# A fifth unit's input product on GpSimd, softplus summed by TensorE, and a re-timed step schedule in a bidirectional selective-scan kernel

## The reference, cut to what matters

```
xp, z   = split(xn @ W_in.T)                     # 512 channels each
xc      = silu(causal_conv4(xp) + b_conv)
dt,B,C  = split(xc @ W_x.T)                      # 16, 16, 16
dt      = softplus(dt @ W_dt.T + b_dt)           # 512 channels
h       = h * exp(dt * A) + (dt * xc) * B        # 512 channels x 16 states, scanned over time
y       = sum over states of h * C, + xc * D
out     = (y * silu(z)) @ W_out.T
```

## Time and profile before

| | us |
|---|---|
| median of 3 runs | 2224.88 (2224.88 to 2226.42) |
| profiled execution, its own time | 2225.93 |
| its span | 2224.2 |
| first scan, last scan's end | 85.2, 1749.3 |
| VectorE busy | 2037.6 (92%) |
| TensorE matmul busy | 1832.9 (82%) |
| GpSimd busy | 1812.6 (81%) |
| ScalarE busy | 1357.1 (61%) |

### The profile page before, as it was taken

The page is one execution under the profiler, slowest core; times in us unless marked ns, Lnnn a source line. Parts: engine busy times, 40 slices in busy tenths (PEclk is TensorE's granted clock), DMA queues, the critical chain, the costliest instruction groups (busy, mean ns, idle before and its releaser), DMA issues.

```text
span 2224.2 us, 24305 instructions
## 1 busy us (share of the span) xinstructions
PE 1832.9 (82%) x6152; PEld 759.6 (34%) x6153; DVE 2037.6 (92%) x2349; ACT 1357.1 (61%) x2442; POOL 1812.6 (81%) x667
## 2 busy tenths in 40 slices
PE   7687787878786979788787878787956699999997
PEld 3222232323231323223232323232312366655554
DVE  7889999999999999999999999999999867657776
ACT  5676758576766667675857676676755243424443
POOL 4489999999999999999999999999999433325444
PEclk9788888989797979888898989797968799999999
DMA  6754434343534445343534353434334462234544
GB/s 253 230 141 107 114 98 120 102 114 98 126 107 98 118 112 121 96 116 102 126 97 114 102 122 105 104 108 119 95 89 119 168 248 101 84 94 81 81 78 67
DMA packets 136495, 259.96 MB, mean 117 GB/s; under 512 B 19984, under 2 KB 42768, under 8 KB 135232
## 3 DMA queue, kind: packets, MB, share of 16 engines
q1 hardware_dynamic: 120064, 230.78, 39.0%
q0 software_dynamic: 13440, 17.93, 4.8%
q10 hardware_dynamic: 2880, 9.96, 1.1%
HBM read 190.32 MB, written 69.34 MB: 117 GB/s over the span
## 4 chain that ended last, share of the span: by engine, by line
DVE 46%; PE 22%; issue 13%; ACT 6%; POOL 5%; DMA 4%; DVEq 3%; SPq 1%; POOLq 0%; ACTq 0%
DVE hst L1457 29%; DVE dbu L1443 9%; PE psum L1995 4%; PE psum L1867 4%; POOL hst L844 3%; PE psum L1806 3%; PE psum L1822 2%; DMA b_rep<-bc_scratch 2%; PE psum L2007 2%; PE psum L1852 2%; ACT psum L1167 1%; DVEq L1696 1%; PE psum L1787 1%; DVE h L1706 1%; DVE h L1718 1%
## 5 line engine op out<-in xcount | busy, mean ns | idle before, releaser
L844 POOL TENSOR_TENSOR hst<-hst,c_rep 128x2048 f32<-128x2048 f32 x255 | 1152.5, 4540 | 25.7 <-ACT state L1155 23.3
L1167 ACT ACTIVATE psum<-dt_rep,neg_a 128x512 f32<-128x512 f32 x1024 | 693.0, 684 | 434.9 <-DVE hst L1457 427.8
L1457 DVE TENSOR_TENSOR_SCAN hst<-psum,state,dbu 128x512 f32<-128x512 f32 x768 | 919.4, 1258 | 0.0
L1443 DVE TENSOR_TENSOR dbu<-psum,b_rep 128x2048 f32<-128x2048 f32 x192 | 434.8, 2265 | 14.5 <-PE psum L1852 14.2
L1852 PE MATMUL psum<-dt,same 32*128 32x512 f32 x384 | 253.0, 743 | 194.5 <-DVE dbu L1443 185.2
L1867 PE MATMUL psum<-hst,same 128*32 128x512 f32 x2048 | 309.6, 759 | 52.1 <-POOL hst L844 43.8
L832 POOL TENSOR_TENSOR dbu<-dtu_rep,b_rep 128x2048 f32<-128x2048 f32 x64 | 291.8, 4560 | 40.4 <-DVE hst L1457 40.4
L1457 DVE TENSOR_TENSOR_SCAN hst<-psum,dbu 128x512 f32<-128x512 f32 x256 | 291.8, 1198 | 6.6 <-ACT psum L1167 6.4
L1806 PE MATMUL psum<-xp,taps 128*128 128x512 f32 x512 | 242.4, 623 | 4.9 <-ACTq L1084 4.9
L965 POOL DMA_INDIRECT out_x<-h,target_u x72 | 114.1, 1585 | 151.6 <-DMA out_x<-h,target_u 78.6
L1852 PEld LDWEIGHTS psum<-dt,same 32*128 32x128 f32 x384 | 64.9, 208 | 341.8 <-DVE dbu L1443 257.7
(11 more groups left out here) (178 smaller groups left out, 2204.3 us busy)
## 6 DMA issues: line engine op xcount, KB each, us to landing
dt_rep<-dt_scratch SPq DMA_DIRECT2D x256, 256.0 KB, 4.7
taps<-taps_scratch SPq DMA_DIRECT2D x64, 256.0 KB, 2.9
b_rep<-bc_scratch SPq DMA_DIRECT2D x64, 256.0 KB, 4.8
dt_scratch<-dt SPq DMA_DIRECT2D x64, 256.0 KB, 2.0
dtu_rep<-dtu_scratch SPq DMA_DIRECT2D x256, 64.0 KB, 1.9
c_rep<-bc_scratch SPq DMA_DIRECT2D x64, 256.0 KB, 7.8
h<-slot_scratch SPq DMA_DIRECT2D x72, 129.5 KB, 2.1
sp_tmp<-t_scratch SPq DMA_DIRECT2D x16, 512.0 KB, 4.7
```

Source lines behind the costliest of these rows:

```text
L844: nc.gpsimd.tensor_tensor(h, h, c_rep[q % 2][:], ALU.mult).then_inc(prod_done, 1)
L1167: nc.scalar.activation(psum[:, PS_A + i, :], dt_rep[:, G % 2, j, :], ACT.Exp, scale=neg_a[:, q % 2, u, i:i + 1]).then_inc(exp_done, 1)
L1443: nc.vector.tensor_tensor(dbu[:, U % DBU, :, :], psum[:, PS_U:PS_U + 1, :].broadcast_to((P, NG, TB)), b_rep[U // UNITS % 2][:], ALU.mult). ...
L1457: nc.vector.tensor_tensor_scan(time_order(hst[:, U % RING, i, :], backward), time_order(psum[:, PS_A + i, :], backward), time_order(dbu[:, ...
```

## The change

Parts:

1. `POOL_UNITS = (3, 7, 9, 11, 15)`: the product of unit 9 moves from VectorE to GpSimd (192 becomes 176 for VectorE, 64 becomes 80 for GpSimd). Its spread input comes by DMA, so `spread_dtu` is called five times a step.
2. The sum of softplus's two parts moves from GpSimd (`add_dt`, gone) to TensorE (`sum_parts`: two products with the identity into one shared bank), and ScalarE copies the sum out (`copy_dt`). The logarithm is taken chunk by chunk.
3. The x projections and convolutions of step q+2 start in units 10 to 15 of step q, those of the next step end by unit 2; the output projection is spread over units 3 and 4; silu of xc moves from (6,3) to (4,3); the copy of `xdbl` moves from (9,1) to (8,3), in front of `silu_z`.
4. Two gates move: chunk 1 to unit 11, chunk 2 behind the first scan of unit 15.
5. SP's order is new, and the DMAs that ScalarE issued in the first units go to SP. `first_units` and the code before the loop are re-timed.

The diff, cut to its core:

```diff
-XP_AT = [(15, 0), (15, 2), (3, 0), (3, 2)]
-CONV_AT = [(2, 1), (2, 2), (5, 1), (6, 0)]
-OUT_AT = [(4, 1), (5, 0)]
-SILU_X_AT = (6, 3)
+CONV1_AT, XP2_AT, XP3_AT, CONV2_AT, CONV3_AT = (0, 1), (0, 3), (1, 0), (2, 0), (4, 0)
+SILU_X_AT = (4, 3)
+OUT_AT = [(5, 0), (6, 0)]
 Z_AT = [(7, 1), (7, 3), (8, 1), (8, 3)]
+XDBL_AT = (8, 3)
 SILU_Z_AT = (8, 3)
-XDBL_AT = (9, 1)
-DT_AT = [(11, 0), (11, 1), (11, 3), (13, 2)]
+DT_AT = [(10, 0), (10, 3), (12, 0), (13, 1)]
+COPY_DT_AT = [(11, 2), (12, 2), (13, 3), (15, 2)]
+XP0_AT, XP1_AT, CONV0_AT = (11, 3), (12, 3), (14, 1)
-LOG_AT = [(11, 3), (13, 3)]
+POOL_UNITS = (3, 7, 9, 11, 15)
...
+        uses += [("conv", q + 1, 1), ("x", q + 1, 2), ("x", q + 1, 3), ("conv", q + 1, 2), ("conv", q + 1, 3)]
+        uses += [("out", q - 1, 0), ("out", q - 1, 1)] + [("z", q, c) for c in range(NC)] + [("xdbl", q + 1, 0)]
+        uses += [("dt", q + 1, 0), ("dt", q + 1, 1), ("sum", q + 1, 0), ("x", q + 2, 0), ("dt", q + 1, 2), ("sum", q + 1, 1)]
+        uses += [("x", q + 2, 1), ("dt", q + 1, 3), ("sum", q + 1, 2), ("conv", q + 2, 0), ("sum", q + 1, 3)]
...
-    return U % GN == GN - 1
+    return U % UNITS in POOL_UNITS
...
             for q in range(STEPS):
+                if q == 0:
+                    store_dt(0, 2)
                 spread_dt(q, 1)
+                if q == 0:
+                    for n in (2, 3, 1):
+                        keep_tokens(n)
+                        keep_turned(n)
...
+                if q > 0:
+                    store_sum(q - 1)
+                spread_dtu(q, 9)
                 if q + 2 < STEPS:
                     load_xnT(q + 2)
+                spread_dtu(q, 11)
...
             def softplus(q, c):
...
+                act.wait_ge(sp_exp, k + 1)
+                nc.scalar.activation(sp_tmp[:, c, :], sp_tmp[:, c, :], ACT.Ln, bias=1.0).then_inc(sp_done, 1)
+            def copy_dt(q, c):
+                bank, free = filled(act, "sum", q, c)
+                nc.scalar.activation(dt[:, c, :], psum[:, bank, :], ACT.Copy).then_inc(free, 1)
...
                     if (t, n) in Z_AT:
                         copy_z(q, Z_AT.index((t, n)))
+                    if (t, n) == XDBL_AT and ahead:
+                        copy_x_dbl(q + 1)
                     if (t, n) == SILU_Z_AT:
                         silu_z(q)
...
-                        if t == 10:
+                        if t == 11:
                             gate_y(q, 1)
-                        if t == 14:
-                            gate_y(q, 2)
+                    if i == 0 and t == 15:
+                        gate_y(q, 2)
                 if t == 8:
                     gate_y(q, 0)
...
+            def sum_parts(q, c):
+                pe.wait_ge(sp_relu, NC * q + c + 1)
+                bank, full = take_bank(pe, "sum", q, c)
+                nc.tensor.matmul(psum[:, bank, :], ident[:], dt[:, c, :], start=True, stop=False)
+                pe.wait_ge(sp_done, NC * q + c + 1)
+                nc.tensor.matmul(psum[:, bank, :], ident[:], sp_tmp[:, c, :], start=False, stop=True).then_inc(full, 1)
...
                     if t == 8:
                         project_xdbl(q + 1)
-                    if t == 10:
+                    if t == 9:
                         project_dt(q + 1, 0)
                         project_dt(q + 1, 1)
...
+                if q > 0 and ahead:
+                    if t == 0:
+                        convolve(q + 1, 2)
+                    if t == 2:
+                        convolve(q + 1, 3)
+                if q > 0:
+                    if t == 3:
+                        project_out(q - 1, 0)
+                    if t == 4:
+                        project_out(q - 1, 1)
...
+                if ahead and t in range(10, 10 + NC):
+                    sum_parts(q + 1, t - 10)
+                if q + 2 < STEPS:
+                    if t == 10:
+                        project_x(q + 2, 0)
+                    if t == 11:
+                        project_x(q + 2, 1)
+                    if t == 12:
+                        convolve(q + 2, 0)
+                    if t == 14:
+                        convolve(q + 2, 1)
+                    if t == 15:
+                        project_x(q + 2, 2)
+                        project_x(q + 2, 3)
```

More of the change, by code:

```diff
@@ L122, in pool_mults @@
 def pool_mults(U):
-    return (U + 1) // GN
+    return len(POOL_UNITS) * (U // UNITS) + sum(u <= U % UNITS for u in POOL_UNITS)
 def keeps_state(U):
@@ L628, in load_sum @@
                         sp.wait_ge(h_stored[n], 16)
-                sp.wait_ge(dt_done, NC * min(q + 1, STEPS - 1) + 2)
+                for c in range(2):
+                    drained(sp, "sum", min(q + 1, STEPS - 1), c)
                 sp.dma_start(t_blk, t_dram[block_of(q)]).then_inc(t_loaded, 16)
@@ L888, in _ @@
             power(LAST, 0)
-            add_dt(0, 0)
+            step_input(0, 0)
             power(LAST, 1)
             shift(LAST)
-            step_input(0, 0)
-            add_dt(0, 1)
             step_input(0, 1)
@@ L1190, in _ @@
             softplus(0, 0)
-            softplus_log(0, 0)
+            copy_dt(0, 0)
+            softplus(0, 1)
             for n in range(2, LATE):
                 turn_copies(n)
-            normalise(5)
-            for c in range(1, NC):
-                softplus(0, c)
-            softplus_log(0, 1)
+            softplus(0, 2)
+            copy_dt(0, 1)
+            copy_xp(1, 0)
             negate_decays()
@@ L1204, in first_units @@
                 if (T, n) == (0, 3):
[L1205 to L1208 removed]
+                    copy_dt(0, 2)
+                    copy_turned(4, 0)
+                    copy_xp(1, 1)
+                    normalise(5)
                 if (T, n) == (1, 0):
[L1210 to L1215 removed]
@@ L1884, in _ @@
                 project_dt(0, c)
+            sum_parts(0, 0)
             for n in range(2, LATE):
                 turn_block(n)
+            turn_xn(4, 0)
+            project_dt(0, 2)
+            sum_parts(0, 1)
             pe.wait_ge(same_set, 8)
-            for c in range(2, NC):
-                project_dt(0, c)
-            for U in range(3):
-                spread_input(U)
-            for c in range(2):
-                project_x(1, c)
+            spread_input(0)
+            project_x(1, 0)
+            sum_parts(0, 2)
+            spread_input(1)
+            turn_xn(4, 1)
+            project_x(1, 1)
+            spread_input(2)
             convolve(1, 0)
-            turn_xn(LATE, 0)
-            TURN_FIRST = {3: (6, 0), 4: (LAST, 0)}
-            TURN_LAST = {0: (4, 1), 1: (5, 0), 2: (5, 1), 3: (6, 1), 4: (LAST, 1)}
+            turn_xn(5, 0)
+            TURN_LAST = {0: (5, 1), 1: (6, 0), 2: (6, 1), 3: (LAST, 0), 4: (LAST, 1)}
             for T in range(ALL_UNITS):
```

254 lines of the change are left out of this document (125 added, 129 removed).

## The result

The kernel after takes 2257.07 us (median of 4 runs, 2255.53 to 2259.15), the kernel before beside it 2225.11 us. The ratio is 1.0143 with an interval of 1.0125 to 1.0161: 32 us slower. The forecast was 2235 us, with a range of 2197 to 2251.

A forecast was written before the change was run, and what follows sets the result against it. VectorE, busy all 104.00 us of a steady step, was taken as the bound. Step 0 -3.6, steps 1, 8, 9 -0.9, eleven steady steps +18.7, step 15 -2.2 gave +12, shaded to +10: 2235 us, range 2197 to 2251.

The forecast's parts named there:

- what bounds the step: VectorE sets the step's length: busy all 104.00 us before, needing 101.8 us without unit 9's product.
- the chain at unit 8: Bank of z(2), `xdbl` passes, its copy, then silu hold the gate of chunk 0: 1.8 us, 3.9 with the clock.
- the clock: TensorE idles 2.6 us before `xdbl`, so its passes run at a lower clock: 2.1 us more, bounds 0 and 3.1.
- rival A: TensorE keeps its clock over the idle before `xdbl`; only the 1.8 us gate wait remains: 2206 us, chance 0.22.
- SP's order at price 0: Unit 9's input, behind `store_sum` on SP, arrives in time for GpSimd: price 0, bounds 0 and 1 us a step.
- step 0 at 3.6 us less: Step 0 was to fall from 112.4 to 108.8 us, bounds 9 less and 4 more.
- I count 6 us of such waits as left: In step 0, waits from ScalarE's layer norms and transposed copies and TensorE's transposes ahead of the spreads: 6 us left.
- the first scan: It was to stay at 85.2 us, where VectorE's norms and its two first products end.
- GpSimd's burst: Products of 7, 9 and 11 still leave unit 12 ready in time: price 0; without the gate's wait, up to 2.1 us a step.
- B: The gate of chunk 0 does not wait, `xdbl`'s matmuls coming earlier: 46 us less, 2179 us, chance 0.12.
- C: Beside the forecast, a 0.9 us wait at the product of unit 16 in most steps: 2248 us, chance 0.15.
- Step 15: The last step has no `xdbl`, so silu ends before the gate needs it: 2.2 us won.

The follow-up runs named there:

- experiment 2: The kernel after with the copy of `xdbl` moved back from (8,3) to (9,1): 2244.62 us.
- experiment 5: The kernel after with three matmuls, read by nobody, in TensorE's idle time before the passes of `xdbl`: 2260.56 us.
- experiment 6: experiment 1 with the order at (8,3) turned round: silu of z, then the copy of `xdbl`, then the exp table load: 2211.52 us.
- experiment 9: experiment 8 with the store of turned block 1 also issued by ScalarE and no longer by SP: 2201.51 us.
- experiment 1: The kernel after with the stores of turned blocks 2 and 3 issued by ScalarE again instead of SP: 2252.36 us.
- experiment 8: experiment 6 with the scaling of the output weights moved from unit 7 to unit 15 of step 0: 2206.85 us.
- experiment 10: experiment 9 with, in step 0, the last turned block copied ahead of softplus and the copy of the sum moved from (6,1) to (6,3): 2200.08 us.
- experiment 11: experiment 10 with two matmuls, read by nobody, in TensorE's idle time before the passes of `xdbl`: 2195.87 us.
- experiment 4: The kernel after with unit 9's product back on VectorE, so four units on GpSimd: 2247.28 us.
- experiment 12: experiment 10 with a GpSimd addition of zero ahead of each product of dt and xc, four a step: 2229.82 us.

## Why the prediction was right and where it was wrong

**Right: what bounds the step, and the chain at unit 8.** VectorE needs 101.85 us (101.8 predicted) and the gate waits 3.65 us (3.9), by the steps named: the bank of z(2), 2.06 us of idle (2.6), the lower clock, the copy ahead of silu. The steady step is 105.5 us (105.7) in eight steps. Experiments 2, 5 and 6 each break the chain at one link; the link at the bank of z(2) is read from the traces alone. Steps 2, 7 and 12 show the part without the clock: the gate waits 1.95 us, where 1.8 was worked out.

The Trainium skill ("ScalarE: Activation LUTs", What ACT_TABLE_LOAD costs) would add a drain of 1.38 us to this wait. The trace after disagrees again: silu starts 1.29 us behind the start of its load (797.57 to 798.86), and leaving the drain out was right.

**Half right: the clock.** The price of 2.1 us was 1.7 where it was paid (5.30 against 3.60), but it wasn't paid in steps 1, 8, 9 and 2, 7, 12. There rival A holds: 100.3 us where it would give 99.9, and 103.8 where it gives 103.6. The steady steps came to +10.3 us instead of +18.7, and steps 1, 8, 9 to -5.9 instead of -0.9. By itself this would have made the forecast too high: with step 0 left out, the kernel after is 1.3 us longer than the kernel before. That the change is clearly slower, which the forecast had from the steady steps, is right by luck; the loss lies elsewhere.

**Wrong, and the reason for the miss: SP's order at price 0, and with it step 0 at 3.6 us less.** The step on SP's order followed one input, that of unit 9, and there it held: VectorE waits for no product of GpSimd. The stores of turned blocks 1 to 3, which the diff moves to SP as well, were not followed: neither what is ahead of them on SP, nor that the copy of a later block waits for their landing. Step 0 came to +28.3 us, 32 off, more than the whole error of 22. The stores of blocks 2 and 3 are 11 us of it, that of block 1 8.6 (experiment 9), and the order at (8,3) 3.1 (129.6 us in experiment 1, 126.5 in experiment 6, with the gate's wait down from 6.7 to 1.9). Another 3.0 us went with the scaling of the output weights (experiment 8), but that stands at unit 7 in the kernel before as well, so it is a gain beside the change and not a part of its cost. "I count 6 us of such waits as left" had no row under it, and its bounds of 9 less and 4 more were for other waits than the one that came. The rest of step 0, 115 against 112.4 us with a first scan 3 us earlier, is small waits for TensorE and ScalarE that experiment 10 could only move; how much of the loss is the earlier copy of block 4, and not the later store, stays open.

**Wrong in a small way: the first scan.** It came at 81.9, not at 85.2; the re-timed code ahead of the loop did win 3.3 us.

**Not tested by the kernel after, and too cheap: the room behind the gate.** "Price 0" for GpSimd's burst ahead of unit 12 held only under the gate's wait, and "up to 2.1 us a step" without it was too little. Once that was gone (experiment 2), VectorE waited up to 3.5 us there; not for GpSimd, but for TensorE at the lower clock. It is why undoing the worst edit brought 12 us and not the 49 expected.

**The rivals.** A: in six steps of sixteen. B (no wait at the gate, 2179 us): false in the kernel after, by 48.8 us of waits; as a kernel it is experiment 6 and those that follow. C (a second wait at the product of unit 16): not in the kernel after; in experiments 6, 8, 10 and 11 it comes with 0.9 to 1.0 us (0.9 worked out), in one to three steps, and in experiment 5 once with 1.5.

**Step 15** won 0.3 us and not 2.2. VectorE's busy time fell from 99.60 to 97.54, and 1.8 us went at the product of unit 12.

**Two slips of arithmetic**, without weight: by the prediction's own pitches VectorE needs 98.0 us without a state, not 97.8 (97.98 measured), and a pass is 3.63/8 = 0.45 us, not 0.43, which makes `sum_parts` 7.3 us a step and not 6.9.

## What to carry to other kernels

Every instruction that a change moves to another queue has two neighbours to follow, what stands ahead of it there and who waits for it to land: 17 us of waiting came from one store that was issued at 90.05 us, with its data ready at 70.19, in the one step that no average shows. Taking work off the engine that bounds the loop shortens the room of every hand-over that was hidden beside it; before crediting the gain, work out which result must now be ready sooner, and put the consumer with the tight date (silu) ahead of the one with time to spare (the copy). And when undoing an edit gives back less than it cost, look for the next wait in the same trace rather than doubt the cause.

## What the runs showed of the hardware

The lower clock comes and goes in the same place of the same kernel. The eight passes of `xdbl` in the kernel after, in steps 2, 6, 7 and 12:

```profile
371.21 3.60 PE L1866 MATMUL psum<-xc,w_x 128*48 128x512 f32 x8 [1.82 <-ACT sz L1105]
791.56 5.30 PE L1866 MATMUL psum<-xc,w_x 128*48 128x512 f32 x8 [2.06 <-ACT sz L1105]
897.08 3.60 PE L1866 MATMUL psum<-xc,w_x 128*48 128x512 f32 x8 [1.92 <-ACT sz L1105]
1412.54 3.60 PE L1866 MATMUL psum<-xc,w_x 128*48 128x512 f32 x8 [1.94 <-ACT sz L1105]
```

In this kernel the passes took 3.60 us in the six steps with 1.17 to 1.94 us of idle ahead of them, at a granted clock of 1.00, and 5.30 in the eight with 2.06 to 2.56, at a mean of 0.68: 1.70 us more, and so whole steps of 103.8 or 105.5 us. But the length of the idle time alone doesn't decide. In step 7 of experiment 1 the passes took 5.30 us behind 1.99 us of idle, in steps 2 and 10 of experiment 10 they took 3.60 behind 2.56. What else counts these runs don't settle. That idle time ahead of the passes matters is shown by experiments 4, 5 and 11: with 0.94 us or less of it they took 3.60 to 3.63 us in every step.

A GpSimd addition of zero from one column broadcast over 128x512 took 1.04 us in the mean, a product of two 128x512 inputs 1.27 (experiment 12).
